# Sixteen expert tiles of 256 rows and seven of 128, and the cross-attention's queries as three rounded passes

## The reference, cut to what matters

```python
x = x + window_attention(layernorm(x))            # windows of 8 tokens, 16 heads of 16
x = x + cross_attention(layernorm(x), ctx_768)    # context 77 x 192, 16 heads of 64
#   q = x @ Wq (256 x 1024); k = ctx @ Wk; v = ctx @ Wv; softmax(q k / 8) v @ Wo + bo
t = layernorm(x)
top1 = argmax(softmax(t @ router_w + router_b))   # one of 8 experts for each token
for i in range(8):
    a, g = split(t @ w1[i] + b1[i])               # w1: 256 x 2048
    y = (a * sigmoid(g)) @ w2[i] + b2[i]          # w2: 1024 x 256
    out += where(top1 == i, y, 0)
x = x + out
```

## Time and profile before

| | before |
|---|---|
| device time, median of 3 (range) | 1249.58 us (1246.37 to 1251.13) |
| the profiled execution: its time, its span | 1249.47 us, 1247.7 us |
| granted TensorE clock, mean | 0.98 |
| busy: TensorE / its weight loads / VectorE / ScalarE / GpSimd | 1150.9 / 976.7 / 841.5 / 604.6 / 653.9 us |
| records of TensorE | 8064 |
| trunk, about 0 to 813 us; experts, about 814 to 1247 us | |

### The profile page before, as it was taken

How to read it: one execution, slowest core, us unless ns; L and a number is a source line. 1 busy time by engine, 2 the same in 40 slices (tenths; PEclk the granted TensorE clock), 3 DMA queues, 4 the chain that set the end, 5 groups by cost and what they waited for, 6 DMA issues and landing times. The chain is left out here.

```text
span 1247.7 us, 22257 instructions
## 1 busy us (share of the span) xinstructions
PE 1150.9 (92%) x8064; PEld 976.7 (78%) x8064; DVE 841.5 (67%) x1501; ACT 604.6 (48%) x1011; POOL 653.9 (52%) x540
## 2 busy tenths in 40 slices
PE   4999699999998999999999999739999999999998
PEld 2655457777777778687777888629999999999997
DVE  3679346777658776568774555328787887788874
ACT  1244423545514545334455555316766666666663
POOL 6548107676548575377675221341655555555643
PEclk9999899999999999999999999859999999999999
DMA  8533301111220111201124114134766576656650
GB/s 190 138 122 123 95 19 45 46 30 47 41 57 22 34 44 25 52 11 46 30 51 138 33 38 139 23 89 149 251 230 221 195 241 214 227 195 214 221 193 5
DMA packets 95463, 133.73 MB, mean 107 GB/s; under 512 B 42410, under 2 KB 76924, under 8 KB 89491
## 3 DMA queue, kind: packets, MB, share of 16 engines
q1 hardware_dynamic: 79379, 111.56, 28.9%
q0 software_dynamic: 16000, 21.07, 6.3%
HBM read 113.31 MB, written 24.73 MB: 111 GB/s over the span
## 5 line engine op out<-in xcount | busy, mean ns | idle before, releaser
L300 POOL TENSOR_TENSOR trunk_space<-staged 128x2048 f32<-128x2048 f32 x27 | 128.4, 4754 | 86.1 <-DVE staged L821 35.2
L1335 PEld LDWEIGHTS psD<-vo,pT 128*128 128x128 f32 x1024 | 124.8, 193 | 24.1 <-issue 20.5
L1335 PE MATMUL psD<-vo,pT 128*128 128x128 f32 x1024 | 134.8, 279 | 6.9 <-issue 5.2
L1572 POOL TENSOR_TENSOR idle<-e_less 128x1 f32<-128x1 f32 x42 | 50.3, 1198 | 170.8 <-DVE ys L1702 90.6
L300 POOL TENSOR_TENSOR trunk_space<-staged,probs 128x2048 f32<-128x2048 f32 x27 | 116.5, 4316 | 28.1 <-DVE probs L854 17.9
L1754 ACT ACTIVATE sig<-psH,b1s 128x256 f32<-128x256 f32 x184 | 77.2, 471 | 109.4 <-PE psH L1820 109.4
L1193 PE MATMUL psA<-xT,wq 128*128 128x256 f32 x512 | 124.1, 391 | 0.7 <-ACT xT L646 0.7
L1687 DVE SCALAR_TENSOR_TENSOR gated<-psH,b1s,sig 128x256 f32<-128x256 f32 x184 | 80.5, 479 | 55.2 <-ACT sig L1754 54.7
L1820 PE MATMUL psH<-xhigh,first_high 128*128 128x256 f32 x384 | 110.7, 288 | 1.5 <-DVE xlow L1680 1.5
L470 POOL TENSOR_TENSOR ve<-mv,eps 128x2 f32<-128x2 f32 x32 | 6.2, 193 | 200.1 <-DVE mv L952 131.6
L732 ACT ACTIVATE pT<-psA 77x512 f32<-77x512 f32 x128 | 76.0, 594 | 69.7 <-PE psA L1317 67.0
(11 more groups left out here) (232 smaller groups left out, 3187.3 us busy)
## 6 DMA issues: line engine op xcount, KB each, us to landing
staged<-in_L_ffn_w SPq DMA_DIRECT2D x69, 1024.0 KB, 5.2
tokens<-out_rows POOLq DMA_DIRECT2D x32, 256.0 KB, 7.3
kT<-k_cols SPq DMA_DIRECT2D x16, 308.0 KB, 3.0
vo<-v_rows SPq DMA_DIRECT2D x16, 308.0 KB
xb<-in_x SPq DMA_DIRECT2D x32, 128.0 KB
b2s<-in_L_ffn_b SPq DMA_DIRECT2D x23, 128.0 KB, 2.7
k_cols<-qT SPq DMA_DIRECT2D x4, 616.0 KB
v_rows<-pT SPq DMA_DIRECT2D x4, 616.0 KB
```

What stands on the lines that cost most here:

```text
L300: done(tensor_tensor(o, a, w, ALU.mult))
L1335: ins = mm(ps[:, m * P:(m + 1) * P], pT[:, (2 * w + m % 2) % 4, (m // 2) * N + t * P:(m // 2) * N + (t + 1) * P], vo[:, 4 * w + m, :], sta ...
L1572: nc.gpsimd.tensor_tensor(idle[:, i:i + 1], e_less_8[:, 0:1], e_less_8[:, 0:1], ALU.add)
```

## The change

1. *Tiles.* The first 16 tiles keep 256 rows, the last 7 have 128 (`BIG`, `SMALL`, `halves`). For a small tile `hidden` uses 128 columns in each of its 96 matmuls, `down` and the turns do one half only, and gather and scatter issue one DMA instead of two. The weights are loaded, rounded and split as before, for all 23 tiles.
2. *Locating.* An expert's tokens are counted in units of 128 rows; its whole pairs and its odd unit are given out to the 16 large and the 7 small tiles. No tile is fixed any more: `locate` computes expert and row for all 23, in about twice as many steps. SyncE therefore loads the first weights after the first part of `locate`, and the ids after the second. Nothing of the experts is loaded, rounded or split in the last group. The shared spaces are gone; `wq` is staged in `oT` and `first_products` use `xnT`.
3. *Queries.* Wq is rounded and split once, near the start (ScalarE after the second pair of contexts, VectorE after the first window scores). In each chunk ScalarE rounds the turned rows (`x_high`), VectorE takes the rest (`x_low`), and each query product is three rounded matmuls. `first_queries` does the passes with `x_high` of the first chunk of 128 columns of queries 0 and 1 before it waits for the split.

The diff, cut to its core:

```diff
-NT = B * N // ET + E - 1
+BIG, SMALL = B * N // ET, E - 1
+NT = BIG + SMALL
...
-            sp.wait_ge(wa_full, NG * WA_ITEMS)
-            for i in range(KC):
-                sp.dma_start(staged[:, i, :], w1[0, i * P:(i + 1) * P, :]).then_inc(w_in[i], 16)
...
+            def queries_rounded(j, b):
+                ps, value = full("XN2'", j, b)
+                then(act, nc.scalar.activation(x_high[:].rearrange("p k n -> p (k n)"), ps, copy), x_rounded, j + 2)
+                nc.scalar.activation(act_idle[:], ident[:, 0:1], copy).then_inc(a_done, 1)
...
+            def split_queries(j, b):
+                item, bank = A("XN2'", j, b)
+                dve.wait_ge(x_rounded, j + 2)
+                then(dve, nc.vector.tensor_tensor(x_low[:].rearrange("p k n -> p (k n)"), psA[:, bank, :],
+                                                  x_high[:].bitcast(F32).rearrange("p k n -> p (k n)"), ALU.subtract),
+                     x_split, j + 2)
...
+            dve.wait_ge(wq_rounded, 1)
+            then(dve, nc.vector.tensor_tensor(wq_low[:], wq, wq_high[:].bitcast(F32), ALU.subtract), wq_split, 1)
...
+            def query_passes(q, u, w, x, j, b, first=False, last=False):
+                ps = psA[:, A(f"Q{q}'", j, b)[1], u * N:(u + 1) * N]
+                cols = slice((2 * q + u) * P, (2 * q + u + 1) * P)
+                for c in range(KC):
+                    ins = mm(ps, w[:, c, cols], x[:, c, :], start=first and c == 0, stop=last and c == KC - 1)
+                return ins
...
+            def first_queries(j, b):
+                pe.wait_ge(x_rounded, j + 2)
+                for q in range(2):
+                    freeA(f"Q{q}'", j, b)
+                    queries_begun(q, 0, j, b)
+                pe.wait_ge(x_split, j + 2)
+                for q in range(2):
+                    query_passes(q, 0, wq_high, x_low, j, b, last=True)
+                    queries_begun(q, 1, j, b)
+                    query_passes(q, 1, wq_high, x_low, j, b, last=True).then_inc(a_full, 1)
...
+        def halves(t):
+            return 2 if not isinstance(t, int) or t < BIG else 1
...
-            load_bias(0, 0)
-            load_bias(1, 1)
+            sp.wait_ge(located, 1)
+            first, second = expert(0), expert(1)
+            for i in range(PIECES):
+                load_piece(0, first, i, wait=False)
+            sp.wait_ge(located, 2)
             for i in range(2):
                 sp.wait_ge(scattered[i], SCATTERED * (B // 2 + 1))
             for t in range(DEPTH):
-                load_ids(t * REGION, t)
+                load_ids(t, t)
+            load_bias(first, 0)
+            load_bias(second, 1)
+            for i in range(PIECES):
+                load_piece(1, second, i)
...
+                n = halves(t) * P
...
-                        passes = [(lhs[par][:, k, w:w + P], rhs[:, par, k, :]) for k in range(KC)
+                        passes = [(lhs[par][:, k, w:w + P], rhs[:, par, k, 0:n]) for k in range(KC)
...
-                    for half in range(2):
+                    for half in range(halves(t)):
```

More of the change, by code:

```diff
@@ L1241, in _ @@
             turn_normed(xn, "XN2'", -1, -1, normed2, 1)
-            queries(0, -1, -1)
-            for q in range(1, 4):
-                queries(q, -1, -1)
+            first_queries(-1, -1)
+            scores_for_max(0, -1, -1)
+            for q in range(2, 4):
+                queries_of(q, -1, -1)
                 scores_for_max(q - 1, -1, -1)
@@ L1404, in turn @@
                     if not last:
-                        queries(0, j, b)
-                        for q in range(1, 4):
-                            queries(q, j, b)
+                        first_queries(j, b)
+                        scores_for_max(0, j, b)
+                        for q in range(2, 4):
+                            queries_of(q, j, b)
                             scores_for_max(q - 1, j, b)
@@ L1572, in carry_waits, with gather @@
                 nc.gpsimd.tensor_tensor(idle[:, i:i + 1], e_less_8[:, 0:1], e_less_8[:, 0:1], ALU.add)
-            def gather(slot, turn, first=None):
+            def gather(t, slot, turn, first=None):
                 pool.wait_ge(ids_in[slot], turn * 16 + 16)
@@ L1611, in _ @@
             for t in range(DEPTH):
-                gather(t, 0, first=True)
+                gather(t, t, 0, first=True)
                 if t == 1:
@@ L1622, in tile @@
                 if exists(t + 4):
-                    gather(slot, turn + 1)
+                    gather(t + 4, slot, turn + 1)
             tiles(pool, tile)
@@ new lines, in locate @@
+                s.done(nc.vector.tensor_scalar(left[:], ends[:, last, 0, E - 1:E], -1.0, float(BIG), ALU.mult, ALU.add))
+                s.done(nc.vector.tensor_scalar(extra[:], parts[:, 1, 1, :], left[:], None, ALU.is_lt))
+                s.done(tt(extra[:], extra[:], parts[:, 0, 1, :], ALU.mult))
+                s.done(nc.vector.tensor_scalar(tiles_of[:, 0, :], parts[:, 1, 0, :], -1.0, float(BIG), ALU.mult, ALU.add))
+                s.done(nc.vector.tensor_scalar(tiles_of[:, 0, :], tiles_of[:, 0, :], 0.0, None, ALU.max))
@@ L1652, in locate @@
+                last = summed(0)
+                for kind, slots in ((0, slice(0, BIG)), (1, slice(BIG, NT))):
+                    n = slots.stop - slots.start
+                    s.done(tt(passed[:, slots], slot_no[:, slots].unsqueeze(2).to_broadcast([P, n, E]),
+                              ends[:, last, kind, :].unsqueeze(1).to_broadcast([P, n, E]), ALU.is_ge))
                 s.done(reduce(tile_e[:], passed[:], axis=X, op=ALU.add))
                 s.done(nc.vector.tensor_scalar(tile_e[:], tile_e[:], float(E - 1), None, ALU.min))
-                then(dve, nc.vector.tensor_copy(tile_ei[:, E:NT], tile_e[:]), located, 1)
+                then(dve, nc.vector.tensor_copy(tile_ei[:], tile_e[:]), located, 1)
@@ L1780, in tile @@
                     gate_high(t + 1, 1)
-            high_part(1, 1, 0)
+            for i in range(KC):
+                high_part(0, 0, i)
             high_tokens(0, 0)
+            high_part(0, 0, KC)
             act.wait_ge(h_done, 2)
```

274 lines of the change are left out of this document (147 added, 127 removed).

## The result

| | before | after |
|---|---|---|
| device time, median of 15 (range) | 1249.6 us (1246.4 to 1251.2) | 1246.3 us (1234.9 to 1260.3) |
| the profiled execution: its time, its span | 1249.5, 1247.7 us | 1235.2, 1233.5 us |
| granted TensorE clock, mean, by run | 0.98 | 0.945 to 0.967 |
| records of TensorE | 8064 | 8138 |

The medians of all fifteen runs differ by 3.3 us, 0.26%. So the change is worth 3 to 7 us. The forecast was 1224 us, 25 us faster. The range 1209 to 1247 held the median, barely.

The account below looks back on a forecast made before the run. TensorE's own instructions were taken to bound queries and tiles, with the change-over priced separately: 1249.5 - 13.5 (queries) + 13 (change-over) - 23.1 (small tiles) - 1.5 (end) = 1224.4, say 1224 us; own range 1216 to 1232, wide range 1209 to 1247.

Parts of the forecast that it names:

- Part 3, small tiles: Seven 128-row expert tiles: narrow hidden matmuls at 0.112 us, each tile 14.2 us instead of 17.5, -23.1 us in all.
- Cheap load: Rival, small tiles: narrow stationary load is quick, hidden matmul falls towards 0.059 us, VectorE sets pace; 1213 us, chance 0.12.
- lost pass: Rival, small tiles: rounded matmul under 256 columns loses its single pass, 0.232 us each; 1302 us, chance 0.16.
- signs of being wrong: Small tiles: hidden-matmul spacing of 0.06 or 0.2 us, or waits for weight splits; each chunk: longer waits for PSUM maxima.
- Part 1, queries: Trunk queries: three rounded passes replace plain matmuls, saving 15.8 us, less 2.3 for splitting Wq: -13.5 us.
- b = 0 and 2: Query chunks that also sum scores or values, VectorE tight: 0.85 us gained in each of six chunks.
- b = 1 and 3: Other query chunks outside the last group: 1.2 us gained in each of six chunks.
- The split of Wq: Start of kernel: VectorE's 128x2048 split stands in the chain that ends last, +2.3 us.
- Part 2, the change-over: Trunk to experts: ids queued behind weights delay the gather and first hidden matmul, +13 us, bounds +3 and +17.
- The end: Last tile: one scatter half instead of two and a shorter last sum, -1.5 us.
- paced by its supply: Rival, small tiles: weight load, rounding and split set the pace, 15.8 us a tile; 1235 us, chance 0.20.
- everything small goes against it: Rival, whole kernel: queries only 6.5 us net, change-over +17, small tiles 15.8 us; 1247 us, chance 0.05.

Follow-up runs that it names:

- the last version: Changed kernel with 256-column hidden matmuls in small tiles, ids of tiles 0 and 1 loaded before weights, last group's clears behind the split: 1221.2 us, ratio 0.9772.

## Why the prediction was wrong

The direction was right, if only just; the size was not: a forecast of 25 us against 3 to 7. The step that failed is the price of a small tile, and by its own steps this is how it came out:

- **Part 3, small tiles.** Its sum was right where the clock is up. A 128-column rounded matmul takes 0.112 us, as taken from the plain logits; a small tile 13.8 us, and the seven tiles without weight loads took 92.1 us where the forecast came to 116.8 - 23.1 = 93.7. Cheap load and lost pass, the rivals at 0.059 and 0.232, are out. What failed is the step that wasn't taken: the price of 0.112 us was used as if it held whatever the clock did. The prediction named the clock only for the change-over ("I leave as it is"). It had said that TensorE sets the pace "but closely"; the supply did come late once, and in the profiled execution 1.9 us of wait became some 14 (tiles of 20.3 and 21.1 us for 13.8 each). At half clock a narrow matmul takes 0.213 us, one of the prediction's signs of being wrong (0.2), but not for the reason it gave, a lost pass. For the median an estimate has to be put together from two runs: 1246.3 against 1226.7, and 2 to 3 us more, which narrow matmuls would have saved at full clock. The clock takes about 22 us there, nearly all that the forecast was off. The groups of times some 11 us apart fit some 27, 50 and 80 us at half clock, which is what their mean clocks come to; whether in one stretch or in several only a trace can tell, and the traces of the narrow kernels have both: single stretches of 27, 48, 79 and 106 us, and once 27 and 48 in one run.
- **Part 1, queries.** Forecast 13.5 us. The run that undoes it says 5 to 7.6, the traces of before and after 7.8 (6.7 up to the last set and 1.1 in it), near or within its bounds of 6 and 22. The spacing was nearly right in the passes (0.120 for 0.118), but the term was mis-sized by what stands around them: an undisturbed set gains 1.13 us (10.68 to 9.55), as forecast at 1.2. With b = 0 and 2 it gains 0.57 where 0.85 was taken, since VectorE's work behind the first maxima has a fixed length; with b = 1 and 3 it gains 0.5 and 0.76 (1.1 in one set) where 1.2 was taken, the split's own price; in the last group's two sets with clears 0.3, forecast 0.4. The first set gave 2.2, forecast 1.5. And 2.9 us came back as waits that no step named: 0.7 us in each of two chunks for VectorE's one-hot rows and 1.6 us once for the window rows. The split of Wq cost 0.2 to 0.9 us instead of 2.3.
- **Part 2, the change-over.** +11.3 us (+10.2 in the table, which has the last set's gain in it), forecast +13, bounds 3 and 17. The mechanism was right: ids issued behind the weights held the gather, and moving them ahead brought the gather 7.6 us forward and the first hidden matmul 3.3. The size was off by two small things: from the pieces' issue to the gather it took 12.7 us and not 14.2, and from the gather to the first hidden matmul 9.3 and not 9.5.
- **The end.** -1.3 us, forecast -1.5.
- **Not in the sum:** -6.7 us for tiles 2 to 16, from the place of two tensors in memory. Without it the change would have been some 3 us slower in the median (an estimate: 1246.3 + 6.7 against 1249.6).

The rival "paced by its supply" came to 1235 us, near the profiled execution, but by another mechanism: tiles are not 15.8 us each, most are 13.8 and some 20 to 26. The sum of "everything small goes against it", 1247 us, is next to the median by luck: its queries came out as it took them, its change-over and its tiles did not. That the stated range held the median is the same luck, since its upper end is that sum.

## What to carry to other kernels

Price a shorter instruction together with the clock: in a stream that waits now and then, halving the columns of a matmul that costs nearly the same anyway (0.112 against 0.117 us) saves 4% of it, and risks the factor 2 of the clock for tens of microseconds. At half clock it saves nothing: both take 0.213 us. When a change makes runs scatter, read the mean granted clock of every run beside its time before reading the one trace. And small loads that start a long chain go ahead of large ones on the same queue.

## What the runs showed of the hardware

- The granted clock fell to 0.50 behind waits of 1.9 us (after, and the last version) and 3.8 us (put in by hand). With wide matmuls it fell behind two of three waits of 1.9 us and behind none of 1.1 to 1.7. With 256-column matmuls it was back after 3.4 us; with the small tiles' stream, four matmuls of 128 columns to each of 256 and no gap, after 27 to 79 us, or not in 106.
- At 1.2 GHz a 128-column rounded matmul takes 0.213 us, as a 256-column one does, and at 2.4 GHz 0.112: what it costs beside its columns goes with the clock too.
- The distance between stationary and moving operand in SBUF, modulo 128 bytes, changes a rounded 256-column matmul from 0.116 (64) to 0.120 us (0), 11 us of this kernel (one run each).
